# Two last iterations of a gated cross-attention block: Wo products in two parts, residual to quantised x by pairs of row tiles, moments of twelve score tiles on ScalarE

## The chip, the cores and the metric

The kernel runs on one core of one Trainium2 chip. The metric is the device time of one execution in microseconds; a row's times are counted from the start of the span of the profiled execution.

## The reference

Eight batches of x and of a context, 512 rows by 512 columns each, float32. Per batch: a layer norm of x, cross-attention with 16 heads of 32 to the context, an output projection, a gated residual, a second layer norm, and a feed-forward layer of 2048 hidden columns with quantised activations and ternary weights. Every head has a temperature of its own, which a small network makes from three features of its scores: mean, mean row maximum, and mean variance of the softmax rows.

```python
x = x + jnp.tanh(g_xattn[0]) * _L0_xattn_ref(_layernorm(x, axis=-1), ctx_1024, ctx_1024, ...)
x = x + jnp.tanh(g_ffn[0]) * _L0_ffn_ref(_layernorm(x, axis=-1), L0_ffn_w1, L0_ffn_w2)
# in _L0_xattn_ref
scores = qk / math.sqrt(dk)
probs = jax.nn.softmax(scores, axis=-1)
entropy_proxy = jnp.var(probs, axis=-1, ddof=1).mean(axis=-1)
...
attn_scores = qk / (2.0 * t)
attn = jax.nn.softmax(attn_scores, axis=-1)
return _linear(out, Wo, bo)
# in _L0_ffn_ref
scale = 127.0 / jnp.clip(jnp.max(jnp.abs(x), axis=-1, keepdims=True), EPS, None)
xq = jnp.clip(jnp.round(x * scale), -128.0, 127.0) / scale
h = jax.nn.gelu(_bitlinear(x, w1), approximate=False)
return _bitlinear(h, w2)
```

## The kernel before

The batches run through three stages that lie beside each other. Iteration i works on batch i + 1 (`has_p`: projections to q, k, v), on batch i (`has_a`: the scores once, for the features; 16 heads by 4 row tiles, 64 "score tiles" of 128 by 512) and on batch i - 1 (`has_b`: the scores again with the temperature, the values, Wo, residual, feed-forward). There are ten iterations, -1 to 8. Iteration 7 has no projections. Iteration 8 has only `has_b`, for the last batch.

Each engine has its own program, in the order in which `body` writes it; an instruction waits on semaphores for the others, and whatever is behind it on its engine waits too. Nothing but this written order decides what comes first.

A score tile is a TensorE product into one of four banks `a_ps` (`score_a`), a row maximum on VectorE (`row_max`, L925), an exponential on ScalarE into one of three slots of `etile` (`first_exp`, L738), and mean and variance of it on VectorE (`row_stat`, L930). The next product into a bank waits for the exponential of four tiles before. `A_PLAN_7` says how many of the 64 tiles of iteration 7 lie in its first part, among the attention of batch 6 ("sets", 48), and how many at each of 16 points behind it. `features` needs all moments.

Behind the sets comes, for batch i - 1:

- `normalise(i - 1, 3, ...)` on VectorE reads out the last chunk of outputs (`o_ps`, L947) and denominators (`z_ps`, L950) and turns the inverse (L957). `split_y` on GpSimd scales the chunk and splits it in two float16 halves, `yT`. There are four chunks, and chunks 0 to 2 were made during the sets.
- The Wo products: for each of four row tiles 12 matmuls (4 chunks, 3 pairs of halves, L1274) and one for the bias (L1277), into banks `b_ps`, `b_ps`, `o_ps`, `z_ps`. TensorE waits for all four chunks ahead of the first.
- `residual` (L1013), `residual_stat` (L986), aggregation (L1202), the reciprocal root on GpSimd (`inverse_deviation`, L621, L623), `norm_residual` (L993), `quantise_x` (L998 to L1004). From the aggregation on each step takes all four row tiles at once.
- Turning the quantised rows on TensorE (L1441), copying them out (row tiles 0 and 2 on VectorE, L1069, 1 and 3 on ScalarE, L839), and the up products of row tile 0 and 1 (`up`, L1450), four banks each of four matmuls, with a Gelu on ScalarE for each (L863). The first Gelu has a table load ahead of it.
- `scale_h` (L1079 and small ones) and `quantise_h` (L1093) on VectorE, turning, down products (L1485), `result` (L1108), and a store of each row tile.

## Time and profile before

| | |
|---|---|
| time, median of 3 runs | 1380.33 us (1379.63 to 1380.57) |
| the profiled execution's own time | 1382.32 us |
| its span | 1380.5 us |
| mean granted TensorE clock | 0.949 |
| busy: PE, DVE, ACT, POOL | 86%, 80%, 67%, 31% |
| chain that ended last | PE 50%, DVE 27%, issue 10%, ACT 8% |

The busy share is a mean over the whole span. A timeline row has the start, the length, the engine (PE is TensorE's matmul, DVE VectorE, ACT ScalarE, POOL GpSimd), the line, the operation with output and input, the count, and in brackets how long the engine was idle just before, and who ended it. Instructions overlap a little, so the distance of two starts is a better price than a length. `region` stands for several buffers.

### The profile page before, as it was taken

The numbers are of one execution on the slowest core, as the hardware profiler recorded it, in microseconds if no ns is written. First come the engines' busy times: TensorE is split into PE (matmuls) and PEld (weight loads), VectorE is DVE, ScalarE is ACT, GpSimd is POOL, SyncE is SP. The second block draws the span as 40 slices with busy tenths as digits, with TensorE's granted clock in tenths as the row PEclk, the third lists the DMA queues.
The fourth block names the chain that finished last, engine by engine and source line by source line (L and its number), as shares of the span: only waits on it lengthen the run. The fifth ranks groups of instructions, "written<-read, shape, count | busy, mean of one in ns | idle before, by whom it ended". The sixth has DMA issues, their size and how long they took to land.

```text
span 1380.5 us, 23490 instructions
## 1 busy us (share of the span) xinstructions
PE 1193.1 (86%) x6684; PEld 440.3 (32%) x6684; DVE 1103.3 (80%) x2054; ACT 922.7 (67%) x1527; POOL 421.9 (31%) x399
## 2 busy tenths in 40 slices
PE   5736669999989899999999999999999999869958
PEld 2202321344214431344224432344224431233224
DVE  6298779988798969897898969897898879983246
ACT  4463579756885769765985669664985679636713
POOL 4279474520253124510253124510353101100210
PEclk9857879999999999999999999999999999979979
DMA  8710221122112221012212221112112210001000
GB/s 295 227 51 11 62 68 38 36 46 62 61 48 47 47 71 54 22 28 62 62 47 47 47 79 47 28 32 58 55 47 46 55 54 1 1 1 62 1 0 31
DMA packets 35473, 73.70 MB, mean 53 GB/s; under 512 B 7952, under 2 KB 7952, under 8 KB 34832
## 3 DMA queue, kind: packets, MB, share of 16 engines
...
## 4 chain that ended last, share of the span: by engine, by line
PE 50%; DVE 27%; issue 10%; ACT 8%; POOL 1%; SPq 1%; DMA 1%; DVEq 1%; ACTq 0%; POOLq 0%
PE b_ps L1274 11%; DVE stat L930 7%; PE o_ps L1485 6%; DVE nmax L925 5%; PE o_ps L1274 5%; PE o_ps L1314 4%; PE z_ps L1274 4%; ACT region L755 4%; PE a_ps L1295 4%; PE b_ps L1301 4%; ACT etile L738 3%; DVE hmax L1079 2%; PE z_ps L1485 2%; PE b_ps L1450 2%; PE z_ps L1325 2%
## 5 line engine op out<-in xcount | busy, mean ns | idle before, releaser
L738 ACT ACTIVATE etile<-a_ps,nmax 128x512 f32<-128x512 f32 x512 | 368.2, 731 | 141.9 <-DVE nmax L925 141.6
L755 ACT ACTIVATE region<-b_ps,inv2t 128x512 f32<-128x512 f32 x512 | 353.3, 754 | 50.0 <-PE b_ps L1301 45.9
L925 DVE TENSOR_REDUCE nmax<-a_ps 128x1 f32<-128x512 f32 x512 | 345.7, 677 | 41.7 <-PE a_ps L1295 37.9
L930 DVE BATCH_NORM_STATS2 stat<-etile 128x6 f32<-128x512 f32 x512 | 347.8, 682 | 12.7 <-ACT etile L738 12.3
L1295 PE MATMUL a_ps<-kst,qst 96*128 96x512 f16 x512 | 202.8, 401 | 60.8 <-ACT etile L738 49.8
L1301 PE MATMUL b_ps<-qst,kst 97*128 97x512 f16 x512 | 192.6, 388 | 20.5 <-DVE region L1102 7.7
L1314 PE MATMUL o_ps<-region,vbuf 128*32 128x512 f32 x1024 | 137.9, 606 | 13.0 <-ACT region L755 7.0
L1325 PE MATMUL z_ps<-region,ones 128*32 128x512 f32 x1024 | 136.2, 604 | 8.4 <-DVE region L950 8.4
L1301 PEld LDWEIGHTS b_ps<-qst,kst 97*128 97x128 f16 x512 | 49.1, 96 | 290.2 <-ACT region L755 258.3
L655 POOL TENSOR_TENSOR region<-region 128x512 f16<-128x512 f32 x64 | 76.0, 1188 | 203.9 <-ACT region L788 203.7
L611 POOL TENSOR_TENSOR region<-region 128x512 f32<-128x512 f32 x32 | 40.8, 1276 | 292.0 <-DVE region L957 292.0
L1079 DVE TENSOR_REDUCE hmax<-region 128x1 f32<-128x512 f32 x128 | 82.2, 680 | 19.5 <-ACT region L863 18.2
L584 POOL CAST c_hi<-cin 128x512 f16<-128x512 f32 x28 | 17.1, 610 | 240.3 <-DMA cin<-in_ctxT_dram 239.5
L1295 PEld LDWEIGHTS a_ps<-kst,qst 96*128 96x128 f16 x512 | 50.7, 100 | 111.9 <-ACT etile L738 57.9
L1485 PE MATMUL o_ps<-f,region 128*128 128x512 fp8e4 x352 | 79.6, 379 | 0.0
L1450 PE MATMUL b_ps<-f,region 128*128 128x512 fp8e4 x256 | 65.3, 394 | 14.8 <-DVE region L1102 12.8
L863 ACT ACTIVATE region<-b_ps,xmax 128x512 f32<-128x512 f32 x64 | 43.4, 689 | 28.1 <-PE b_ps L1450 27.7
L632 POOL TENSOR_SCALAR cin<-cin,mv,rstd 128x512 f32<-128x512 f32 x28 | 57.9, 2077 | 2.8 <-POOL rstd L623 2.6
L873 ACT ACTIVATE region<-b_ps 128x1024 f16<-128x1024 f16 x31 | 31.7, 1023 | 32.0 <-PE b_ps L1461 31.2
L947 DVE TENSOR_SCALAR region<-o_ps 128x512 f32<-128x512 f32 x32 | 21.7, 680 | 36.9 <-PE o_ps L1314 36.9
L621 POOL TENSOR_SCALAR rstd<-mv 128x2 f32<-128x2 f32 (+1 forms) x23 | 5.3, 232 | 143.4 <-DVE mv L1202 87.4
L1274 PE MATMUL b_ps<-wo_hi,region 128*128 128x512 f16 x128 | 43.4, 399 | 5.7 <-POOL region L616 5.7
...
## 6 DMA issues: line engine op xcount, KB each, us to landing
kst<-region SPq DMA_DIRECT2D x96, 128.0 KB, 2.3
qst<-region SPq DMA_DIRECT2D x96, 128.0 KB, 2.3
...
```

The costliest lines, as they stand in the source:

```text
L738: nc.scalar.activation(etile[:, k % E_SLOTS, :], a_ps[k % A_BANKS][:, :], ACT.Exp, bias=nmax[:, slot_of(n), t:t + 1], scale=1.0).then_inc( ...
L755: nc.scalar.activation(probs[:, (s + 1) % 2, g, :], b_ps[g % 2][:, :], ACT.Exp, scale=inv2t[:, slot:slot + 1]).then_inc(b_exp, 1)
L925: vec.tensor_reduce(nmax[:, slot_of(k // T), k % T:k % T + 1], a_ps[k % A_BANKS][:, :], AX.X, ALU.max, negate=True).then_inc(a_max, 1)
L930: vec.bn_stats(stat[:, slot_of(k // T) * T + k % T, :], etile[:, k % E_SLOTS, :]).then_inc(a_stat, 1)
L1079: ins = vec.tensor_reduce(hmax[:, n:n + 1], hbuf[t % 2][:, n * S:(n + 1) * S], AX.X, ALU.max, apply_absolute_value=True)
L1274: ins = mat(mm_ps[bank_n][:, :], left[l](c), right[r](c), start=(c, l, r) == pairs[0], stop=bias is None and (c, l, r) == pairs[-1])
L1295: mat(a_ps[k % A_BANKS][:, :], qst[par][0:SHIFT, slot, t * P:(t + 1) * P], kst[par][0:SHIFT, slot, :], start=True, stop=True).then_inc(a_f ...
L1301: mat(b_ps[g % 2][:, :], kst[par][0:SHIFT + 1, slot, k * P:(k + 1) * P], qst[par][0:SHIFT + 1, slot, :], start=True, stop=True).then_inc(b ...
L1314: ins = mat(o_ps[g * DK:(g + 1) * DK, :], vbuf[par][:, k, n * DK:(n + 1) * DK], probs[:, (s + 1) % 2, g, :], start=k == 0, stop=k == T - 1)
L1325: ins = mat(z_ps[g * DK:(g + 1) * DK, :], ones32[:, 0:DK], probs[:, (s + 1) % 2, g, :], start=k == 0, stop=k == T - 1)
L1450: ins = mat(mm_ps[bank_n][:, :], xqT[:, c, t * P:(t + 1) * P], f1[:, c, n * S:(n + 1) * S], start=c == 0, stop=c == C - 1)
L1485: ins = mat(mm_ps[bank_n][:, :], hT[t % 2][:, k, :], f2[:, k, :], start=k == 0, stop=k == KC - 1)
```

## The change

It touches iterations 7 and 8 alone.

1. The Wo products of both iterations come in parts. `w_part(t, chunks)` makes chunks 0 to 2 of row tiles 0, 1 and 2 as soon as these chunks are there; then, when the last is, the rest of tiles 0 and 1, all of tile 3, and the rest of tile 2.
2. In iteration 7 the 16 tiles behind the sets move from points 0 to 7, two each, to the first six points, as 3, 3, 3, 3, 2, 2. The first nine of them now stand between the parts.
3. Residual to quantised x goes by pairs of row tiles (`stat_pair`, `quantise_pair`; the reciprocal root too). Turning pair 0 and its copies stand ahead of the up products of row tile 0, those of pair 1 ahead of the up products of row tile 1. ScalarE makes all four copies.
4. Moments of the last twelve tiles of batch 7 (`by_act`): ScalarE sums the exponentials as it makes them and squares them in place with a sum; three small VectorE instructions (`stats_by_act`) put mean and square sum where `features` reads them.
5. In iteration 8 a Gelu of a small, unused tile stands behind the last exponential.

```diff
@@ -50,16 +50,25 @@
-A_PLAN_7 = (48, (2, 2, 2, 2, 2, 2, 2, 2, 0, 0, 0, 0, 0, 0, 0, 0))
+A_PLAN_7 = (48, (3, 3, 3, 3, 2, 2, 0, 0, 0, 0, 0, 0, 0, 0, 0, 0))
...
+def by_act(i, k):
+    return isinstance(i, int) and (i == 7 and k >= H * T - 3 * T)
+BY_ACT = sum(by_act(7, k) for k in range(H * T))
...
+LINKS_END = 12
@@ -735,15 +753,33 @@
+                if k >= E_SLOTS and by_act(b, k - E_SLOTS):
+                    act_waits.wait_ge(squared, squares_by(b, k - E_SLOTS))
+                at = slot_of(n) * T + t
...
-                                     bias=nmax[:, slot_of(n), t:t + 1], scale=1.0).then_inc(a_exp, 1)
+                                     bias=nmax[:, slot_of(n), t:t + 1], scale=1.0,
+                                     accum_out=stat[:, at, 1:2] if by_act(b, k) else None).then_inc(a_exp, 1)
+            def squares_by(b, k):
+                return sum(by_act(b, n) for n in range(k + 1))
+            def square(b, k):
+                at = slot_of(k // T) * T + k % T
+                act_waits.wait_ge(a_exp, nth(b, H * T, k + 1))
+                nc.scalar.activation(etile[:, k % E_SLOTS, :], etile[:, k % E_SLOTS, :], ACT.Square,
+                                     accum_out=stat[:, at, 2:3]).then_inc(squared, 1)
             def late_exp(b, k):
...
+                if k > E_LATE and by_act(b, k - E_LATE - 1):
+                    square(b, k - E_LATE - 1)
...
+                    for late in range(H * T - E_LATE - 1, H * T):
+                        if by_act(b, late):
+                            square(b, late)
@@ -873,9 +912,14 @@
+                if has_b and not has_a:
+                    nc.scalar.activation(expt[:, :], expt[:, :], ACT.Gelu)
...
-                    gelus(0)
-                    gelus(1)
+                    for t in range(2):
+                        if not has_p:
+                            turned_xq(2 * t)
+                            turned_xq(2 * t + 1)
+                        gelus(t)
@@ -926,8 +970,25 @@
             def row_stat(b, k):
+                if by_act(b, k):
+                    return
+                covered = 1
+                while k + covered < H * T and by_act(b, k + covered):
+                    covered += 1
...
-                vec.bn_stats(stat[:, slot_of(k // T) * T + k % T, :], etile[:, k % E_SLOTS, :]).then_inc(a_stat, 1)
+                vec.bn_stats(stat[:, slot_of(k // T) * T + k % T, :], etile[:, k % E_SLOTS, :]).then_inc(a_stat, covered)
+            def stats_by_act(i):
+                by_tile = stat[:, :, :].rearrange("p (h t) f -> p h t f", t=T)
+                own = by_tile[:, 2 * C - 1::C, :, :]
+                mean, mean_too, rest = (own[:, :, :, f] for f in (1, 4, 5))
+                dve_waits.wait_ge(squared, BY_ACT)
+                vec.tensor_scalar(mean, mean, 1.0 / S, None, ALU.mult).then_inc(act_link, 1)
+                dve_waits.wait_ge(act_link, 1)
+                vec.tensor_copy(mean_too, mean)
+                vec.scalar_tensor_tensor(out=rest, in0=mean, scalar=-float(S), in1=mean,
+                                         op0=ALU.mult, op1=ALU.mult).then_inc(act_link, 1)
+                dve_waits.wait_ge(act_link, 2)
@@ -1005,6 +1066,31 @@
+            def stat_pair(i, pair, c):
+                for t in (2 * pair, 2 * pair + 1):
+                    ins = residual_stat(i, t)
+                c.link(ins)
+                for t in (2 * pair, 2 * pair + 1):
+                    ins = vec.bn_aggr(mv2[:, t, :], st6[:, t, :])
+                ins.then_inc(mv2_pair, 1)
+            def quantise_pair(i, pair, c):
+                cols = slice(2 * pair, 2 * pair + 2)
+                dve_waits.wait_ge(mv2_pair, nth(i - 8, 2, pair + 1))
+                dve_waits.wait_ge(rstd2_pair, nth(i - 8, 2, pair + 1))
+                for t in (2 * pair, 2 * pair + 1):
+                    ins = vec.tensor_scalar(xq[:, t, :], xres[:, t, :], mv2[:, t, 0:1], rstd2[:, t:t + 1],
+                                            ALU.subtract, ALU.mult)
+                c.link(ins)
+                c.link(vec.tensor_reduce(xmax[:, 0, cols], xq[:, cols, :], AX.X, ALU.max, apply_absolute_value=True))
+                c.link(vec.tensor_scalar(xmax[:, 0, cols], xmax[:, 0, cols], EPS, None, ALU.max))
+                vec.tensor_scalar(xmax[:, 3, cols], xmax[:, 0, cols], s1_127[:, 0:1], None, ALU.mult)
+                c.link(vec.reciprocal(xmax[:, 1, cols], xmax[:, 0, cols]))
+                c.link(vec.tensor_scalar(xmax[:, 2, cols], xmax[:, 1, cols], 127.0, None, ALU.mult))
+                for t in (2 * pair, 2 * pair + 1):
+                    vec.tensor_scalar(xq[:, t, :], xq[:, t, :], xmax[:, 2, t:t + 1], MAGIC,
+                                      ALU.mult, ALU.add).then_inc(xq_done, 1)
@@ -1089,6 +1175,9 @@
+                    dve_waits.wait_ge(mm_full[bank_n], before + 1)
+                elif not stages(i)[2]:
+                    bank_n, before = mm_use(i, "xq", T - 1)
@@ -1187,15 +1276,28 @@
-                if has_b:
+                if has_b and has_p:
...
-                for t in range(T):
+                elif has_b:
+                    c = Chain(dve_waits, end_link, LINKS_END, i - 8)
+                    residual(i, 0)
+                    residual(i, 1)
+                    stat_pair(i, 0, c)
+                    residual(i, 2)
+                    tiles_a(C)
+                    quantise_pair(i, 0, c)
+                    residual(i, 3)
+                    stat_pair(i, 1, c)
+                    tiles_a(C + 1)
+                    quantise_pair(i, 1, c)
+                    c.end()
+                for t in range(T) if has_p or not has_b else ():
...
-                if has_b:
+                if has_b and has_p:
@@ -1363,17 +1467,41 @@
-                    if has_b and n == 2:
+                    if has_b and has_p and n == 2:
...
-                    else:
+                    elif not has_b:
...
-                if has_b:
+                def w_part(t, chunks):
+                    bank_n = take(i, "W", t) if chunks[0] == 0 else mm_use(i, "W", t)[0]
+                    for c in chunks:
+                        for l, r in ((0, 0), (0, 1), (1, 0)):
+                            mat(mm_ps[bank_n][:, :], yT[:, l, c, t * P:(t + 1) * P], (w_hi, w_lo)[r]["o"][:, c, :],
+                                start=(c, l, r) == (0, 0, 0), stop=False)
+                    if chunks[-1] == C - 1:
+                        mat(mm_ps[bank_n][:, :], ones16[:, :], bias16[:, 1, :], start=False, stop=True) \
+                            .then_inc(mm_full[bank_n], 1)
+                if has_b and not has_p:
+                    pe_waits.wait_ge(y_done, nth(i - 1, C, C - 1))
+                    for t in range(T):
+                        if t == 2:
+                            pe_waits.wait_ge(o_out, nth(i - 1, C, C))
+                            pe_waits.wait_ge(z_out, nth(i - 1, C, C))
+                        if t == T - 1:
+                            pe_waits.wait_ge(y_done, nth(i - 1, C, C))
+                            w_part(0, (C - 1,))
+                            w_part(1, (C - 1,))
+                        w_part(t, range(C - 1) if t < T - 1 else range(C))
+                        alone(tiles_a(t))
+                    w_part(T - 2, (C - 1,))
+                    alone(tiles_a(C) + tiles_a(C + 1))
+                elif has_b:
...
-                for t in range(T):
+                for t in range(T) if has_p or not has_b else ():
@@ -1486,12 +1617,17 @@
-                    for t in range(T):
+                    for t in range(T) if has_p else ():
...
-                    up(0)
-                    up(1)
+                    for t in range(2):
+                        if not has_p:
+                            turned_xq(2 * t)
+                            turned_xq(2 * t + 1)
+                            drained(i, "xq", 2 * t)
+                            drained(i, "xq", 2 * t + 1)
+                        up(t)
```

TensorE's program in iteration 7, from the last denominators (`z_ps`) of the sets on; `a_ps` is a score tile, `b_ps0` with `wo` the Wo product of row tile 0. Before:

```order
L1325 MATMUL z_ps<-region1,ones32 32x512 x4
L1295 MATMUL a_ps0<-kst1,qst1 128x512
L1295 MATMUL a_ps1<-kst1,qst1 128x512
L1295 MATMUL a_ps2<-kst1,qst1 128x512
L1295 MATMUL a_ps3<-kst1,qst1 128x512
L1295 MATMUL a_ps0<-kst1,qst1 128x512
L1295 MATMUL a_ps1<-kst1,qst1 128x512
L1295 MATMUL a_ps2<-kst1,qst1 128x512
L1295 MATMUL a_ps3<-kst1,qst1 128x512
L1295 MATMUL a_ps0<-kst1,qst1 128x512
L1274 MATMUL b_ps0<-wo_hi,region4 128x512
L1274 MATMUL b_ps0<-wo_lo,region4 128x512
```
and now:

```order
L1429 MATMUL z_ps<-region1,ones32 32x512 x4
L1482 MATMUL b_ps0<-wo_hi,region4 128x512
L1482 MATMUL b_ps0<-wo_lo,region4 128x512
L1482 MATMUL b_ps0<-wo_hi,region4 128x512 x2
L1482 MATMUL b_ps0<-wo_lo,region4 128x512
L1482 MATMUL b_ps0<-wo_hi,region4 128x512 x2
L1482 MATMUL b_ps0<-wo_lo,region4 128x512
L1482 MATMUL b_ps0<-wo_hi,region4 128x512
L1399 MATMUL a_ps0<-kst1,qst1 128x512
L1399 MATMUL a_ps1<-kst1,qst1 128x512
L1399 MATMUL a_ps2<-kst1,qst1 128x512
L1482 MATMUL b_ps1<-wo_hi,region4 128x512
```
Nine matmuls of Wo have moved ahead of the first of these score tiles, and the tiles stand in threes between the parts.

ScalarE's program in iteration 7, its end of the score tiles up to the first Gelus; `etile` from `a_ps` is an exponential, `etile` from `etile` a square, `region3` a copy of turned x, `region4` a Gelu. Before:

```order
L738 ACTIVATE etile<-a_ps2,nmax 128x512
L738 ACTIVATE etile<-a_ps3,nmax 128x512
L839 ACTIVATE region3<-b_ps1 128x4x128
L839 ACTIVATE region3<-z_ps 128x4x128
L863 ACT_TABLE_LOAD
L863 ACTIVATE region4<-b_ps0,xmax 128x512
```
and now:

```order
L759 ACTIVATE etile,stat<-a_ps2,nmax 128x512
L769 ACTIVATE etile,stat<-etile 128x512
L759 ACTIVATE etile,stat<-a_ps3,nmax 128x512
L769 ACTIVATE etile,stat<-etile 128x512 x2
L856 ACTIVATE region3<-b_ps0 128x4x128
L856 ACTIVATE region3<-b_ps1 128x4x128
L902 ACT_TABLE_LOAD
L902 ACTIVATE region4<-o_ps,xmax 128x512
L902 ACTIVATE region4<-z_ps,xmax 128x512
L902 ACTIVATE region4<-b_ps0,xmax 128x512
L902 ACTIVATE region4<-b_ps1,xmax 128x512
```
Each tile has gained a square, behind the exponential of the next one, and all of these stand ahead of the copies. There is one table load, where it was.

VectorE's program in iteration 8, from the first residual on. Before:

```order
L1013 SCALAR_TENSOR_TENSOR xres<-b_ps0,tg_w,xres 128x512
L1013 SCALAR_TENSOR_TENSOR xres<-b_ps1,tg_w,xres 128x512
L986 BN_STATS st6<-xres 128x6
L1013 SCALAR_TENSOR_TENSOR xres<-o_ps,tg_w,xres 128x512
L986 BN_STATS st6<-xres 128x6
L1013 SCALAR_TENSOR_TENSOR xres<-z_ps,tg_w,xres 128x512
L986 BN_STATS st6<-xres 128x6 x2
L1202 BN_AGGR mv2<-st6 128x2 x4
L993 TENSOR_SCALAR region1<-xres,mv2,rstd2 128x512 x4
L998 TENSOR_REDUCE xmax<-region1 128x4
L999 TENSOR_SCALAR xmax<-xmax 128x4
L1000 TENSOR_SCALAR xmax<-xmax,s1_127 128x4
```
and now:

```order
L1099 SCALAR_TENSOR_TENSOR xres<-b_ps0,tg_w,xres 128x512
L1099 SCALAR_TENSOR_TENSOR xres<-b_ps1,tg_w,xres 128x512
L1047 BN_STATS st6<-xres 128x6 x2
L1074 BN_AGGR mv2<-st6 128x2 x2
L1099 SCALAR_TENSOR_TENSOR xres<-o_ps,tg_w,xres 128x512
L1082 TENSOR_SCALAR region1<-xres,mv2,rstd2 128x512 x2
L1085 TENSOR_REDUCE xmax<-region1 128x2
L1086 TENSOR_SCALAR xmax<-xmax 128x2
L1087 TENSOR_SCALAR xmax<-xmax,s1_127 128x2
L1088 RECIPROCAL xmax<-xmax 128x2
L1089 TENSOR_SCALAR xmax<-xmax 128x2
L1091 TENSOR_SCALAR region1<-region1,xmax 128x512 x2
```
The four residuals and four moments ahead of the aggregation have become two and two, the third residual stands between the first pair's aggregation and its normalising, and maximum and rounding take two row tiles.

## Rows read from the trace of the kernel before

**Rows 1.** Busy time in two stretches: length, PE, PEld, DVE, ACT, POOL, PEclk, DMA
```profile
1184.00:1212.00 28.00, 18.34 (x76) 6.90 (x68) 26.93 (x50) 10.99 (x16) 3.58 (x5) 0.84 0.00 1
1309.00:1342.00 33.00, 16.77 (x79) 7.47 (x72) 15.59 (x33) 2.48 (x3) 4.29 (x5) 0.76 0.00 0
```

**Rows 2.** Timeline of DVE, iteration 7: start, length, engine, line, operation, count, idle before
```profile
1186.11 0.69 DVE L925 TENSOR_REDUCE nmax<-a_ps 128x1 f32<-128x512 f32 x1
...
1188.51 0.69 DVE L957 STREAM_TRANSPOSE region<-zinv 128x512 f32<-128x512 f32 x1
...
1208.93 0.73 DVE L1013 SCALAR_TENSOR_TENSOR xres<-z_ps,tg_w,xres 128x512 f32<-128x512 f32 x1
1209.59 1.27 DVE L986 BATCH_NORM_STATS2 st<-xres 128x6 f32<-128x512 f32 x2
1210.89 0.38 DVE L1202 BATCH_NORM_AGGREGATE mv<-st 128x2 f32<-128x6 f32 x4
1212.83 1.91 DVE L993 TENSOR_SCALAR region<-xres,mv,rstd 128x512 f32<-128x512 f32 x4 [1.55 <-POOL rstd L623]
1214.78 2.29 DVE L998 TENSOR_REDUCE xmax<-region 128x4 f32<-128x2048 f32 x1
...
1217.85 1.67 DVE L1004 TENSOR_SCALAR region<-region,xmax 128x512 f32<-128x512 f32 x4
...
1234.70 1.29 DVE L1093 TENSOR_SCALAR region<-region,hsc 128x2048 f32<-128x2048 f32 x1
```

**Rows 3.** Timeline of PE, iteration 7
```profile
1184.52 1.04 PE L1295 MATMUL a_ps<-kst,qst 96*128 96x512 f16 x4
...
1221.23 3.57 PE L1450 MATMUL b_ps<-f,region 128*128 128x512 fp8e4 x8 [0.95 <-DVE region L1069]
```

**Rows 4.** Timeline of ACT, iteration 7
```profile
1220.32 0.60 ACT L839 ACTIVATE region<-z_ps 128x512 f16<-128x512 f16 x1 [0.26 <-PE z_ps L1441]
1220.93 1.28 ACT L863 ACT_TABLE_LOAD   x1
```

**Rows 5.** Timeline of ACT, iteration 6: an activation whose sum is read back
```profile
1031.74 0.69 ACT L784 ACTIVATE region<-b_ps,bqk 128x512 f32<-128x512 f32 x1
1032.32 0.19 ACT L784 ACTIVATION_READ_ACCUMULATOR region<-b_ps,bqk 128x1 f32 x1
1032.42 0.68 ACT L788 ACTIVATE region<-b_ps,bqk 128x512 f16<-128x512 f32 x1
```

**Rows 6.** Timeline of PE, iteration 8
```profile
1308.56 1.04 PE L1325 MATMUL z_ps<-region,ones 128*32 128x512 f32 x8
1315.34 0.58 PE L1274 MATMUL b_ps<-wo_hi,region 128*128 128x512 f16 x1 [5.74 <-POOL region L616]
...
1328.29 0.38 PE L1277 MATMUL z_ps<-bias,ones 128*128 128x512 f16 x1
...
1341.04 3.57 PE L1450 MATMUL b_ps<-f,region 128*128 128x512 fp8e4 x8 [0.98 <-DVE region L1069]
...
1373.65 3.62 PE L1485 MATMUL z_ps<-f,region 128*128 128x512 fp8e4 x16
```

**Rows 7.** Timeline of all engines, iteration 8
```profile
1311.13 0.71 DVE L957 STREAM_TRANSPOSE region<-zinv 128x512 f32<-128x512 f32 x1
...
1347.43 0.69 ACT L863 ACTIVATE region<-z_ps,xmax 128x512 f32<-128x512 f32 x1 [0.39 <-PE z_ps L1450]
...
1349.76 1.29 DVE L1093 TENSOR_SCALAR region<-region,hsc 128x2048 f32<-128x2048 f32 x1
...
1354.34 1.29 DVE L1093 TENSOR_SCALAR region<-region,hsc 128x2048 f32<-128x2048 f32 x1
```

**Rows 8.** TensorE's clock in stretches of 1 us (PEclk, third from the end)
```profile
1189.00:1190.00 1.00, 0.16 (x1) 0.00 (x0) 1.00 (x3) 0.18 (x1) 0.71 (x1) 0.80 0.00 0
...
1196.00:1197.00 1.00, 1.00 (x5) 0.44 (x4) 1.00 (x3) 0.50 (x2) 0.00 (x0) 0.79 0.00 0
1312.00:1313.00 1.00, 0.00 (x0) 0.00 (x0) 0.00 (x0) 0.00 (x0) 1.00 (x1) 0.74 0.00 0
```

53 lines of the change are left out of this document (34 added, 19 removed).

## The prediction

> **What bounds the kernel now.** I read the stages first, then each engine's timeline in them, and last the clock. Everything ahead of the last score tiles of iteration 7 keeps its instructions, so only two stretches matter.
>
> In iteration 7 the stretch from 1184 to 1212 is VectorE's: it is busy 26.93 of 28.00 us, ScalarE 10.99 [rows 1]. From 1186.11 it takes a maximum and a moment for each of 16 tiles, 0.60 us an instruction (four between 1186.11 and 1188.51), with the residual work between them. Then comes a chain with nothing beside it: aggregation at 1210.89, reciprocal root on GpSimd, normalising at 1212.83, maximum at 1214.78, rounding at 1217.85 [rows 2], turning, copying, and the first up product at 1221.23 [rows 3].
>
> In iteration 8 no engine is the bound from 1309 to 1342: TensorE 16.77, VectorE 15.59 of 33.00 us [rows 1]. It is one chain: denominators end about 1309.5, TensorE stands 5.74 us until GpSimd has split the last chunk of y, Wo runs 1315.34 to 1328.67, and the first up product starts at 1341.04 [rows 6]. The clock adds to it: it fell during 1312 to 1313 and Wo began at the lower level, 1.2 GHz, as did the up products (8 in 3.57 us against 16 in 3.62 us at the full 2.4 GHz) [rows 6, 8]. The chain from an up product to the rounding of h of tile 1 (1354.34) is the last place where the instructions differ in order; behind it TensorE runs nearly without gaps [rows 7].
>
> **The change in iteration 8**, on the clock of before. Three quarters of each of three Wo products, 27 matmuls at 0.216 us, 5.8 us, go into the gap from 1309.5: to 1315.3. TensorE has come straight from dense work, so I take the full clock. The last chunk is ready when it was, 4.21 us after the transposition at 1311.13, at 1315.34 [rows 6, 7]. Then 4, 4, 13 and 4 matmuls: tiles 0, 1, 3 and 2 are full at 1316.4, 1317.3, 1320.1 and 1320.9. The last was full at 1328.67: 7.8 us earlier.
>
> VectorE: residual of tiles 0 and 1 at 1316.5 and 1317.35 (0.66 each), moments 1.27 from 1318.0, two aggregations 0.2 to 1319.5. The root takes GpSimd and hand-overs 1.56 (1210.89 plus 0.38 to 1212.83) and is ready at 1321.05; residual 2 stands ahead in the order and waits for its bank until 1321.0, to 1321.65. Two normalisings 1.0, maximum of two tiles 1.2 (half of 2.29, a bound above is two row maxima of 0.69, 1.4), five small ones 0.8 (1214.78 plus 2.29 to 1217.85), rounding 0.5 and 0.9 [rows 2]: tile 1 is rounded at 1325.5. Turning takes 0.8 (rounded at 1219.52, the copy at 1220.32), ScalarE's copy 0.60, the hand-over 0.31 (1220.92 to 1221.23) [rows 2 to 4]: up product of tile 0 at 1327.2, against 1341.04: 13.8 earlier. TensorE was idle for over 4 us before, so I keep the half clock here.
>
> Now the price. Tile 1's up product waits for row tiles 2 and 3. They are rounded by 1333.0 (residual at 1325.4, then the same steps), hidden by the first up product; but their copies stand on ScalarE behind four Gelus. The fourth Gelu starts 6.39 us after the up product, as before (1341.04 to 1347.43), at 1333.6; two copies end at 1335.3; up product of tile 1 at 1335.6. Its 16 matmuls take 3.6, and from the start of the last Gelu to the rounding of h are 2.33 us (1347.43 to 1349.76) [rows 6, 7]: rounding of tile 1 at 1341.6 instead of 1354.34, **12.7 us** gained. Of 13.8 about 1.1 is given back. The dummy Gelu moves the 1.28 us table load behind the last exponential, where ScalarE waits some 15 us. I cost it at nothing and credit it with nothing: where it stood, the load ran beside the first up product, whose four matmuls take 1.9 us at the half clock [rows 4, 6]; at the full clock it would have been 0.3 late.
>
> **The change in iteration 7.** Nine Wo matmuls, 1.9 us, now stand ahead of tile 48, which started at 1184.52 [rows 3]; VectorE, free at 1186.11, gets it at 1186.9. That costs 0.8. Then six tiles with both instructions and two without moments until tile 56, at 1196.5; the transposition is at 1190.5, so the last y chunk is ready at 1194.7 (4.21 later). 21 matmuls, 4.5 us, stand before tile 57: VectorE gets it at 1199.55, having waited 3 us. Maxima 57 to 59, residuals 0 and 1, moments, aggregation, residual 2, maxima 60 and 61: 1206.1. Pair 0 is rounded at 1209.8, residual 3, moments and aggregation to 1211.9, and only then maximum 62, done at 1212.65, and 63.
>
> ScalarE's new work is twelve sums at exponentials and twelve squares. No square stands in the trace. An activation with its sum read back is followed by the next after 0.68 us (1031.74 to 1032.42) [rows 5]; the bounds are 0.60, the plain copy [rows 4], and 0.88, if 0.69 and 0.19 did not overlap. I take 0.68, the same shape. Twelve moments of 0.60 leave VectorE, 7.2 us; 16.3 us arrive on ScalarE, which had 17 idle. It is through tile 61's exponential by 1208 and waits for maximum 62 at any of these prices. Behind that are two exponentials and three squares, 3.4 us (3.1 to 4.4), to 1216.05, then two copies to 1217.15, and the up product at 1217.45: 3.8 earlier. As in iteration 8, copies 2 and 3 wait for four Gelus (1223.85), tile 1's up product starts at 1225.85, its rounding is at 1231.9 instead of 1234.70 [rows 2]: **2.8 us**. The three small VectorE instructions that finish ScalarE's moments, about 0.8, and the features end near 1221.7, before the Gelus need VectorE.
>
> Here the Trainium skill, in "ScalarE: Activation LUTs", What ACT_TABLE_LOAD costs, puts a switch at 2.66 us, a load of 1.28 and a drain of 1.38. The load agrees with the 1.28 of [rows 4]. By that figure, an estimate, the first Gelu of iteration 7 would start 0.45 us later, and the fourth, on which the sum rests, not at all.
>
> **Sum.** 12.7 and 2.8 are 15.5 us. The profiled execution took 1382.32 us (span 1380.5); 1366.8 then, and as the median of the runs was 2.0 lower, 1380.33, I predict **1364.8 us**.
>
> **Rivals.**
> - Both gains as above: 62%, 1362.8 to 1367.0, the width being the bounds of squares and maxima and a microsecond of where the clock rises.
> - The clock falls in iteration 7. Between 1191.7 and 1194.7 TensorE has only two score tiles, and with such sparse work it fell during 1189 to 1190, to rise during 1196 to 1197 after 3.4 us of dense work [rows 8]. 21 matmuls at half the clock for those 3.4 us cost 1.7 to 2.0 us, all ahead of tile 57 and so on the chain: 1366.8. For it: both falls came 3 to 4 us after dense work. Against: three bursts lie closer together now. 18%.
> - Iteration 7 gives nothing, because ScalarE's squares, its waits on itself and the late maximum 62 add up to 2.8 us more: 1367.6. 7%.
> - The clock is full at iteration 8's up product. The first Gelu then follows the copies, but rounding of tiles 2 and 3 (1333.0) holds the next: 1.0 more, 1363.8. 7%.
> - The Wo parts do not run ahead in iteration 8, held by a bank or by the fourth chunk: then only the pairs gain, 12.7 less 7.8: 1372.6. 3%. I see no such wait, the banks being read out by 1310.4.
> - Slower: the square needs another table than the exponential. From tile 53 on they alternate, 21 switches of 1.28 us are 27 us, less some 7 in which ScalarE waits: 20 onto the chain, 1385. From 18 switches on the kernel is slower. Against it: the instruction order has no load among them. 2%. By the 2.66 us a switch of the Trainium skill, "ScalarE: Activation LUTs", an estimate, it would be near 1414; the section Table sets: the hidden batching unit of the same page of the Trainium skill has the cheap functions in every set, and no run here shows a square yet.
> - The remaining 1% is no change.
>
> What a measurement of this kernel tells from none is 0.2%, 2.8 us: slower 2%, same 1%, faster 97%. 1361.5 to 1369.5 leaves out the last three cases and tails of the first.
>
> **What would show it.** Right: the first Wo matmul of iteration 8 directly behind the denominators, about 0.1 us instead of 5.74, and Wo at the full clock; last Wo product to first up product about 6.3 us instead of 12.4; in iteration 7 a ScalarE gap before the exponential of tile 62 and the up product 3.8 us earlier, but h of tile 1 only 2.8. Wrong: a square much over 0.7 us, table loads between L759 and L769, Wo matmuls 0.43 us apart in iteration 7, VectorE waiting over 4 us for tile 57, or a pair's chain longer than 4.0 us from normalising to the second rounding.

## The result, and the profile after

The changed kernel takes 1365.22 us (median of 4 runs, 1362.88 to 1366.75), the kernel before 1380.45 (4 runs beside it): ratio 0.9878, 95% interval 0.9862 to 0.9894. Of 1380.33 that is 16.8 us less (14.6 to 19.0); the medians differ by 15.2, which lies inside that. The prediction was 1364.8, range 1361.5 to 1369.5, a gain of 15.5. The profiled execution is the quickest of the four, 1362.88 us with a span of 1360.9, so its profile shows more gain than the median. One of the runs of parts_8 below, 1587.31 us at a granted clock of 0.745, is a slow one and is left out.

The same two stretches in the changed kernel; iteration 8's lies 6 us earlier. Columns as in [rows 1].

```profile
1184.00:1212.00 28.00, 16.43 (x73) 6.82 (x71) 23.80 (x49) 16.14 (x45) 4.91 (x7) 0.82 0.00 0
1303.00:1336.00 33.00, 26.11 (x136) 11.71 (x128) 24.57 (x57) 10.42 (x17) 4.92 (x7) 0.90 0.00 0
```

VectorE has 3.1 us less in the first stretch and ScalarE 5.2 more; in the second TensorE's busy share rose from half to four fifths, with the same length of window. Where the time went is seen in the timelines. First TensorE in iteration 8, the counterpart of [rows 6]:

```profile
1303.56 0.39 PE L1482 MATMUL b_ps<-wo_hi,region 128*128 128x512 f16 x1
...
1314.57 0.38 PE L1485 MATMUL o_ps<-bias,ones 128*128 128x512 f16 x1
1319.42 1.01 PE L1542 MATMUL b_ps<-ident,region 128*128 128x128 f16 x8 [4.47 <-DVE region L1091]
1321.23 1.86 PE L1581 MATMUL o_ps<-f,region 128*128 128x512 fp8e4 x4 [0.80 <-ACT region L856]
...
1328.47 1.89 PE L1581 MATMUL b_ps<-f,region 128*128 128x512 fp8e4 x8 [1.19 <-ACT region L856]
```

The 5.74 us of idle are gone: Wo follows the denominators directly (their last row starts at 1302.58 and Wo at 1303.56), 0.216 us a matmul throughout, and from its end (1314.95) to the first up product are 6.3 us. VectorE's timeline in the same place, the counterpart of [rows 7]:

```profile
1305.15 0.71 DVE L1018 STREAM_TRANSPOSE region<-zinv 128x512 f32<-128x512 f32 x1
...
1334.70 1.29 DVE L1182 TENSOR_SCALAR region<-region,hsc 128x2048 f32<-128x2048 f32 x1
```

ScalarE's timeline there:

```profile
1301.66 1.28 ACT L916 ACT_TABLE_LOAD   x1
...
1320.04 1.08 ACT L856 ACTIVATE region<-b_ps 128x512 f16<-128x512 f16 x2 [16.87 <-PE b_ps L1542]
...
1326.71 0.69 ACT L902 ACTIVATE region<-b_ps,xmax 128x512 f32<-128x512 f32 x1 [0.18 <-PE b_ps L1581]
```

The table load follows the last exponential; the unused Gelu comes behind it at 1302.96, and 16.87 us of waiting behind that. The copies of pair 1 stand behind the fourth Gelu, and TensorE waits 1.19 for them ahead of the up product of tile 1.

VectorE in iteration 7, against [rows 2]:

```profile
1182.44 0.69 DVE L1008 TENSOR_SCALAR region<-o_ps 128x512 f32<-128x512 f32 x1
...
1185.60 0.69 DVE L969 TENSOR_REDUCE nmax<-a_ps 128x1 f32<-128x512 f32 x1 [0.88 <-PE a_ps L1399]
...
1193.35 1.86 DVE L969 TENSOR_REDUCE nmax<-a_ps 128x1 f32<-128x512 f32 x3
1198.15 1.89 DVE L969 TENSOR_REDUCE nmax<-a_ps 128x1 f32<-128x512 f32 x3 [2.94 <-PE a_ps L1399]
...
1210.53 1.26 DVE L969 TENSOR_REDUCE nmax<-a_ps 128x1 f32<-128x512 f32 x2
...
1214.86 0.88 DVE L1091 TENSOR_SCALAR region<-region,xmax 128x512 f32<-128x512 f32 x2
1215.66 0.17 DVE L986 TENSOR_SCALAR stat<-stat 128x12 f32<-128x12 f32 x1
...
1228.72 1.29 DVE L1182 TENSOR_SCALAR region<-region,hsc 128x2048 f32<-128x2048 f32 x1
...
1235.27 0.68 DVE L1191 TENSOR_SCALAR region<-b_ps 128x1024 f16<-128x1024 f16 x1
```

It waits 2.94 us for tile 57 and makes the last two maxima at 1210.53. ScalarE there, against [rows 4, 5]: exponential with its sum, square with its sum, the late maximum, the copies and the table load.

```profile
1193.55 0.62 ACT L769 ACTIVATE etile<-etile 128x512 f32<-128x512 f32 x1
1194.07 0.19 ACT L769 ACTIVATION_READ_ACCUMULATOR etile<-etile 128x1 f32 x1
1194.16 0.68 ACT L759 ACTIVATE etile<-a_ps,nmax 128x512 f32<-128x512 f32 x1
...
1194.82 0.62 ACT L769 ACTIVATE etile<-etile 128x512 f32<-128x512 f32 x1
...
1211.22 0.69 ACT L759 ACTIVATE etile<-a_ps,nmax 128x512 f32<-128x512 f32 x1 [4.46 <-DVE nmax L969]
...
1214.40 1.07 ACT L856 ACTIVATE region<-b_ps 128x512 f16<-128x512 f16 x2
1215.49 1.28 ACT L902 ACT_TABLE_LOAD   x1
1217.48 0.69 ACT L902 ACTIVATE region<-o_ps,xmax 128x512 f32<-128x512 f32 x1 [0.70 <-PE o_ps L1581]
```

TensorE there, against [rows 3]:

```profile
1208.34 1.01 PE L1542 MATMUL b_ps<-ident,region 128*128 128x128 f16 x8 [5.46 <-DVE region L1091]
1215.57 1.86 PE L1581 MATMUL o_ps<-f,region 128*128 128x512 fp8e4 x4 [6.22 <-ACT region L856]
...
1222.74 1.89 PE L1581 MATMUL b_ps<-f,region 128*128 128x512 fp8e4 x8 [1.35 <-ACT region L856]
```

And the clock of the changed kernel, in stretches of 1 us (third figure from the end):

```profile
1196.00:1197.00 1.00, 1.00 (x6) 0.49 (x5) 0.00 (x0) 1.00 (x5) 0.00 (x0) 1.00 0.00 0
...
1202.00:1203.00 1.00, 0.61 (x1) 0.10 (x1) 0.96 (x4) 0.82 (x4) 0.07 (x1) 0.54 0.00 0
...
1219.00:1220.00 1.00, 1.00 (x6) 0.47 (x5) 0.93 (x4) 0.69 (x1) 0.00 (x0) 0.93 0.00 0
...
1324.00:1325.00 1.00, 1.00 (x4) 0.31 (x3) 1.00 (x1) 0.16 (x1) 0.00 (x0) 0.52 0.00 0
```

Two such stretches of the kernel before, where its clock rose:

```profile
1227.00:1228.00 1.00, 1.00 (x5) 0.39 (x4) 0.69 (x1) 0.44 (x2) 0.00 (x0) 0.93 0.00 0
...
1346.00:1347.00 1.00, 1.00 (x4) 0.39 (x3) 0.06 (x1) 0.64 (x1) 0.00 (x0) 0.69 0.00 0
```

It stayed at 2.4 GHz through iteration 7's Wo and fell to 1.2 at 1202.1, just ahead of the last score tile. The share of a stretch at the higher level gives the moment of a rise: 3.6 us (1219.1) and 3.7 us (1325.0) after the first up product began (1215.57, 1321.23); before, 5.9 and 5.6 (1227.1 and 1346.6 against 1221.23 and 1341.04). These differences do not belong to the change. In iteration 7 of only_8 and of parts_8, two kernels of the experiments that have the code of before there, the clock rose 5.5 us and 3.3 us after the up product (1222.26 and 1223.09). The stretch of parts_8:

```profile
1226.00:1227.00 1.00, 1.00 (x5) 0.44 (x4) 0.90 (x5) 0.37 (x1) 0.00 (x0) 0.81 0.00 0
```

**One measure for all runs.** The tail of iteration 7 begins at different times in runs of identical code ahead (1182.3 to 1187.4 in the fourteen profiles). So I count from VectorE's readout of the last chunk of y (the 1182.44 row; in iteration 8 the like one at 1302.83), in us: to the first up product, to the rounding of h of tile 1, and in iteration 7 to VectorE's copy of the second turned h (the 1235.27 row) and to TensorE's first scores for iteration 8. These are differences of starts in the timelines. "Rise" is how long after the first up product the clock rose to 2.4 GHz, from stretches of 0.1 us; "full" where it was there already. The kernels are those of the experiments.

| kernel | 7: up | rise | h of tile 1 | second copy | scores | 8: up | rise | h of tile 1 |
|---|---|---|---|---|---|---|---|---|
| before | 37.43 | 5.9 | 50.90 | 57.44 | 69.32 | 32.23 | 5.6 | 45.53 |
| changed | 33.13 | 3.6 | 46.28 | 52.83 | 64.70 | 18.40 | 3.7 | 31.87 |
| only_8 | 37.46 | 5.5 | 50.74 | 57.29 | 69.17 | 18.20 | 5.8 | 32.42 |
| only_7 | 33.13 | 4.0 | 46.49 | 53.04 | 64.92 | 33.01 | 3.0 | 45.04 |
| parts_8 | 37.69 | 3.3 | 49.86 | 56.41 | 68.45 | 25.72 | 3.8 | 38.13 |
| pairs_8 | 37.47 | 3.0 | 49.48 | 56.02 | 67.90 | 24.07 | full | 37.75 |
| dve_moments | 34.72 | 5.7 | 49.86 | 56.40 | 68.28 | 18.40 | 3.9 | 31.87 |
| four_early | 28.92 | 5.1 | 46.22 | 52.77 | 64.65 | 18.40 | 4.5 | 31.98 |
| busy_8 | 33.14 | 3.1 | 46.06 | 52.61 | 64.49 | 18.01 | full | 32.94 |
| best | 31.55 | full | 46.21 | 52.76 | 64.64 | 18.01 | full | 32.94 |
| late_3 | 28.90 | 4.5 | 46.22 | 54.16 | 67.28 | 18.39 | 4.6 | 32.06 |
| late_2 | 28.90 | 5.2 | 42.88 | 54.14 | 67.63 | 18.40 | 5.0 | 32.25 |
| late_1 | 33.14 | 3.6 | 46.27 | 57.53 | 70.64 | 18.40 | 4.6 | 32.06 |
| late_all | 28.91 | 5.2 | 42.87 | 52.58 | 65.61 | 18.40 | 3.6 | 31.88 |

So iteration 8 gained 13.66 us, iteration 7 4.62, and 1.36 of the spans' 19.6 is only that the tail began at 1182.44 and not 1183.80. Part of this is the clock's luck in this pair of profiles. Iteration 7's unchanged code gave 49.48 to 50.90 in four profiles, in the order of its rises (3.0, 3.3, 5.5, 5.9), and the changed code 46.06 to 46.49 in four (changed, only_7, busy_8, late_1), again in the order of the rises (3.1 to 4.0). The gain of iteration 7 is therefore 3.0 to 4.8, and 3.4 to 3.8 at like rises of 3.0 to 3.3; the changed order of iteration 7 was never seen with a late one. In iteration 8 the gain is 13.1 at late rises (before and only_8: 45.53 less 32.42) and 13.2 at early ones (only_7 and changed: 45.04 less 31.87). Together 16.5 to 17.0, which fits the 16.8 of the ratio.

### The profile page after: what moved, and what is told of

Read it like the earlier page. It is cut to its first block, busy times and chain, and to the rows that moved or that the text cites. A ratio compares the mean times of both kernels' runs of the same rounds, so it can differ in the third digit from the quotient of the medians.

```text
span 1360.9 us, 23535 instructions
## 1 busy us (share of the span) xinstructions
PE 1185.5 (87%) x6684; PEld 438.3 (32%) x6684; DVE 1097.6 (81%) x2051; ACT 932.9 (69%) x1568; POOL 424.0 (31%) x403
## 3 DMA queue, kind: packets, MB, share of 16 engines
q8 instruction: 62, 1.02, 0.3%
## 4 chain that ended last, share of the span: by engine, by line
PE 50%; DVE 27%; issue 10%; ACT 9%; POOL 1%; SPq 1%; DMA 1%; DVEq 1%; ACTq 0%; POOLq 0%
PE b_ps L1378 10%; DVE stat L979 7%; DVE nmax L969 6%; PE o_ps L1616 6%; PE o_ps L1378 5%; PE o_ps L1418 4%; ACT region L791 4%; PE b_ps L1405 4%; PE z_ps L1378 4%; PE a_ps L1399 4%; ACT etile L759 3%; DVE hmax L1165 2%; PE z_ps L1616 2%; PE z_ps L1429 2%; PE b_ps L1581 2%
## 5 line engine op out<-in xcount | busy, mean ns | idle before, releaser
L979 DVE BATCH_NORM_STATS2 stat<-etile 128x6 f32<-128x512 f32 x500 | 339.9, 683 | 12.5 <-ACT etile L759 12.1
L1165 DVE TENSOR_REDUCE hmax<-region 128x1 f32<-128x512 f32 x128 | 82.1, 680 | 12.7 <-ACT region L902 11.4
L1581 PE MATMUL b_ps<-f,region 128*128 128x512 fp8e4 x256 | 62.2, 380 | 14.3 <-DVE region L1191 11.7
L1616 PEld LDWEIGHTS o_ps<-f,region 128*128 128x128 f16 x352 | 33.8, 98 | 38.0 <-issue 1.1
```

The costliest lines, as they stand in the source:

```text
L979: vec.bn_stats(stat[:, slot_of(k // T) * T + k % T, :], etile[:, k % E_SLOTS, :]).then_inc(a_stat, covered)
L1165: ins = vec.tensor_reduce(hmax[:, n:n + 1], hbuf[t % 2][:, n * S:(n + 1) * S], AX.X, ALU.max, apply_absolute_value=True)
L1581: ins = mat(mm_ps[bank_n][:, :], xqT[:, c, t * P:(t + 1) * P], f1[:, c, n * S:(n + 1) * S], start=c == 0, stop=c == C - 1)
L1616: ins = mat(mm_ps[bank_n][:, :], hT[t % 2][:, k, :], f2[:, k, :], start=k == 0, stop=k == KC - 1)
```

## The experiments

Each is timed beside the kernel before, in four groups, each group on one chip: only_8, only_7, dve_moments and four_early; parts_8, pairs_8, busy_8 and best; late_3, late_2 and late_1; late_all. The ratio is to the kernel before of the same group, whose medians were 1382.41, 1382.01, 1382.53 and 1381.42 us. Gains in us are the ratio's of 1380.33. Each ratio has an interval of about 2 us either way, so differences between kernels of under 3 us rest on the table.

### Which iteration, which part

The edits are the changed kernel's parts behind switches: Wo in parts, pairs, point table, ScalarE's moments, the early Gelu.

```diff
-                if has_b and not has_p:
+                if parts(i):          # Wo in parts
...
-                if has_b and has_p:
+                if has_b and not pairs(i):   # whole residual, as before
...
-    return isinstance(i, int) and (i == 7 and k >= H * T - 3 * T)
+    return isinstance(i, int) and (i == 7 and k >= H * T - BY_ACT_HEADS * T)
# only_8:  table of before, IN_PARTS = (8,), IN_PAIRS = (8,), BY_ACT_HEADS = 0, early Gelu
# only_7:  new table, IN_PARTS = (7,), IN_PAIRS = (7,), BY_ACT_HEADS = 3, no early Gelu
# parts_8: table of before, IN_PARTS = (8,), IN_PAIRS = (), BY_ACT_HEADS = 0, no early Gelu
# pairs_8: table of before, IN_PARTS = (), IN_PAIRS = (8,), BY_ACT_HEADS = 0, no early Gelu
```

**only_8.** 

> Iteration 7 as before the change, iteration 8 as after it. By the prediction's sum iteration 8 holds 12.7 of the 15.5 us: 12.7 faster than before, 1367.7, or up to 1 us more where the clock rises early in the first up products, as it did in the profile of the changed kernel. Rival: iteration 7 holds more than its 2.8 us, as that profile's 4.6 between the two readouts suggests, and iteration 8 under 11.5 of the measured 15.2. It also shows whether the two gains add: this run and the one with iteration 7 alone should together be faster than before by 15 to 16 us.

Measured: 1369.73 us, ratio 0.9907 (0.9891 to 0.9922), 12.8 us; iteration 8 by the table 13.1. Here the clock rose late, as in the kernel before, which is the case that the prediction was worked out for: the up product came 14.0 earlier, the fourth Gelu 6.48 us behind it (1327.85 to 1334.33; forecast 6.39), and 0.9 was given back (forecast 1.1).

**only_7.** 

> Iteration 7 as after the change, iteration 8 as before it. Prediction's sum: 2.8 us faster than before, 1377.6; with the clock rising 1.7 us earlier in the up products, as in the profile of the changed kernel, 4.5 us, 1375.9. Rival: the squares on ScalarE and the late maximum of tile 62 eat it up, 0 to 1 us faster, 1380.

Measured: 1377.61 us, ratio 0.9968 (0.9954 to 0.9983), 4.4 us; by the table 4.4. The two add up: 17.2 of the change's 16.8.

**parts_8.** 

> The kernel before with one thing of the change: in iteration 8 the Wo products in parts. Neither pairs nor the early Gelu. The last product is full 7.8 us earlier by the prediction, but all four steps still wait for it, in the order 0, 1, 3, 2, so residual 2 and its moment come behind it: 7.8 to 8.0 us faster than before, 1372.5. Rival: the 27 matmuls that run ahead do not run at the full clock, 1.9 to 4 us less: about 1375.

Measured: 1374.19 us (five runs), ratio 0.994 (0.9926 to 0.9954), 8.3 us; by the table 7.4. The last Wo product is full 7.7 us earlier, but the first up product comes only 6.5 earlier: residual 2 now waits for that product, and it and its moment stand ahead of residual 3 and the aggregation, 1.26 us that the kernel before had hidden beside Wo (TensorE stands 10.76 us ahead of turning, before 9.50). That h of tile 1 still gains 7.4 is the early rise of the clock (3.8 against 5.6); against iteration 8 of only_7, with a rise at 3.0, it is 6.9.

**pairs_8.** 

> The kernel before with one thing of the change: in iteration 8 residual to quantised x by pairs, and all copies on ScalarE. Wo as before, so it is full at 1320.25, 1323.06, 1325.86, 1328.67. Pair 0 starts 5.6 us before the last product and is through before it; pair 1 starts where all four did, takes about 1.5 us less on VectorE, and its copies stand behind four Gelus. By adding: 12.7 less 7.8 is 4.9 us faster, 1375.5. If pairs in Wo's old, slower order let pair 0 run wholly beside Wo, the gain is larger, 6 to 7 us, and the parts and the pairs do not add. Rival: nothing, since the last copy, not the first, starts the feed-forward: 1379 to 1380.

Measured: 1374.19 us, ratio 0.9946 (0.9932 to 0.996), 7.5 us; by the table 7.8, where 4.9 was what my sum left for it. The parts alone and the pairs alone make 15.2, both together 13.7, or 14.2 and 13.2 against iteration 8 of only_7, where the clock rose early too. The timelines of TensorE show the difference. With parts alone, the first up product:

```profile
1332.42 1.03 PE L1567 MATMUL b_ps<-ident,region 128*128 128x128 f16 x8 [10.76 <-DVE region L1090]
...
1335.26 3.57 PE L1606 MATMUL b_ps<-f,region 128*128 128x512 fp8e4 x8 [0.95 <-DVE region L1180]
```

With pairs alone:

```profile
1330.86 0.61 PE L1567 MATMUL b_ps<-ident,region 128*128 128x128 f16 x8 [1.67 <-DVE region L1116]
...
1332.46 1.02 PE L1606 MATMUL o_ps<-f,region 128*128 128x512 fp8e4 x4 [1.00 <-ACT region L881]
```

With pairs alone the residual of pair 0 hides beside Wo's later tiles, TensorE stands only 1.67 us and the up product runs at the full clock (4 matmuls in 1.02 us); with the parts too, Wo is over sooner, TensorE stands 4.47 and the up product runs at half (1.86). Each part takes something that the other would also have given. The early Gelu has no run of its own, so that it gives nothing is argued and not shown.

### ScalarE's moments

```diff
-    return isinstance(i, int) and (i == 7 and k >= H * T - 3 * T)
+    return isinstance(i, int) and (i == 7 and k >= H * T - BY_ACT_HEADS * T)   # BY_ACT_HEADS = 0: no tile
```

**dve_moments.** 

> The changed kernel with all 64 moments of batch 7 on VectorE again: no sums at exponentials, no squares. Theory: VectorE gets 12 moments of 0.60 back; three hide in its wait for tile 57, nine do not, and those ahead of tile 62 delay the last exponentials, behind which the copies stand; five sums and squares fewer stand behind tile 62. Net 1.9 us slower than the changed kernel, 1367.1. Rival: the squares stand on the chain themselves (three of 0.62 behind tile 62's maximum) and moving moments gained nothing: 0 to 1 us faster than the changed kernel.

Measured: 1368.73 us, ratio 0.9898 (0.9884 to 0.9913), against 0.9878 of the change: 2.8 us slower, and 3.6 in iteration 7 by the table. The 2.8 alone would not be clear of noise; beside four_early, timed on the same chip, its five runs (1366.84 to 1371.90) all lie above those four (1362.98 to 1366.25). With its moments on VectorE iteration 7 has 49.86, inside the 49.48 to 50.90 of the unchanged one: parts and pairs alone give it 0 to 1 us, though the up product comes 2.7 earlier. Its gain is the work that left VectorE. It is less than the 7.2 us of the twelve moments, since part of them hides in VectorE's waits: that for tile 57 is 1.15 us here against 2.94, those for Gelus are gone, and the small three are not needed.

### The late maximum and the clock

```diff
-A_PLAN_7 = (48, (3, 3, 3, 3, 2, 2, 0, 0, 0, 0, 0, 0, 0, 0, 0, 0))
+A_PLAN_7 = (48, (3, 3, 3, 3, 4, 0, 0, 0, 0, 0, 0, 0, 0, 0, 0, 0))
```

**four_early.** 

> The changed kernel with the last four score tiles of batch 7 together, all ahead of the rounding of pair 0, instead of two there and two behind the aggregation of pair 1. Theory: what holds the first up product of iteration 7 is the maximum of tile 62 (ScalarE idle 4.46 us in the profile, then two exponentials and three squares, then the copies). The pair 0 chain gets 1.2 us longer, ScalarE is through before it, the first up product starts about 3.5 us earlier and that of tile 1 about 2.8: 1362.4. Rival: VectorE's own chain is the bound, 1.2 us slower than the changed kernel, 1366.4.

Measured: 1365.0 us, ratio 0.9877 (0.9861 to 0.9893): as the change. The first up product came 4.2 us earlier, and h of tile 1 was rounded at 46.22 against 46.28. My reason, the late maximum as the bound, fell. VectorE shows what held it: behind the rounding of pair 1 come features and both tiles' maxima of h with no idle time, and TensorE waits for it. VectorE's timeline in four_early:

```profile
1224.10 1.29 DVE L1207 TENSOR_SCALAR region<-region,hsc 128x2048 f32<-128x2048 f32 x1
1225.30 2.46 DVE L1190 TENSOR_REDUCE hmax<-region 128x1 f32<-128x512 f32 x4
...
1228.68 1.29 DVE L1207 TENSOR_SCALAR region<-region,hsc 128x2048 f32<-128x2048 f32 x1
```

TensorE's timeline there, behind the up product of tile 1:

```profile
1225.44 1.07 PE L1617 MATMUL b_ps<-ident,region 128*128 128x128 f16 x16 [2.56 <-DVE region L1207]
```

In the changed kernel two chains end almost together here: this one and ScalarE's Gelus behind the late copies, for which VectorE waits four times by 0.18 us. And four_early opens a wait of its own: the last two maxima no longer stand between the aggregation of pair 1 and its normalising, and VectorE waits 1.21 us there for GpSimd's root.

```profile
1213.06 1.00 DVE L1107 TENSOR_SCALAR region<-xres,mv,rstd 128x512 f32<-128x512 f32 x2 [1.21 <-POOL rstd L662]
```

```diff
...
+                            for n in range(WARM[i]):       # WARM = {8: 20}
+                                mat(a_ps[0][:, :], ident16[:, :], w_hi["o"][:, 0, :], start=True, stop=True)
...
                             turned_xq(2 * t)
```

**busy_8** adds these matmuls, whose results nobody reads, ahead of the first transposes of iteration 8. 

> The changed kernel, and in iteration 8 twenty more matmuls of 128 by 512 into an unused bank, between the last Wo product and the first turning, whose results nobody reads: 4.3 us at 2.4 GHz in a gap of 4.6. Theory: they keep the clock up, the first up products of iteration 8 run at 0.22 instead of 0.43 us a matmul, but the rounding of pair 1 then holds the up product of tile 1: 1.0 us faster, 1364.2, with less spread between runs. Rival: the clock at the first up products costs nothing that shows, or the added matmuls delay the turning: same to 1 us slower.

Measured: 1368.15 us, ratio 0.9891 (0.9875 to 0.9907), no gain (its five runs go from 1364.31 to 1368.68). TensorE:

```profile
1325.05 1.02 PE L1606 MATMUL o_ps<-f,region 128*128 128x512 fp8e4 x4 [0.82 <-ACT region L881]
...
1330.70 0.40 PE L1567 MATMUL o_ps<-ident,region 128*128 128x128 f16 x4 [2.04 <-DVE region L1116]
...
1332.32 3.57 PE L1606 MATMUL b_ps<-f,region 128*128 128x512 fp8e4 x8 [0.82 <-ACT region L881]
```

Tile 0's up product ran at the full clock, then TensorE stood 2.04 us for pair 1's rounding and 0.82 for a copy, the clock fell at 1332.3, and tile 1's up product ran at half: h of tile 1 at 32.94, 1.07 later than in the change. The half clock had been moved by one product. In pairs_8 the same two waits were 1.85 and 0.83 and the clock stayed up; what decides between them is open.

**best** joins four_early, busy_8 and 24 such matmuls in iteration 7. 

> The changed kernel with the last four score tiles together ahead of pair 0's rounding, and added matmuls ahead of the first turning in both iterations (24 in iteration 7, 20 in iteration 8). Theory: 2.8 us for the tiles, 1.0 for the clock in iteration 8 and up to 2.5 for it in iteration 7, where the first up products then run at the full clock and pair 1 becomes the bound: 1359 to 1361. Rival: the added matmuls collide with turning in iteration 7, where the gap depends on ScalarE: not better than the tiles alone.

Measured: 1365.19 us, ratio 0.9878 (0.9864 to 0.9892): as the change. In iteration 7 the rival was seen: the 24 matmuls took 7.52 us, and the first up product came 2.6 us later than in four_early, though at the full clock. Yet h of tile 1 was rounded at 46.21, as in four_early and the change. Over these three the up product lies anywhere from 28.92 to 33.13 and that rounding does not move: VectorE sets it.

### VectorE's order in iteration 7

If VectorE's order holds the tail, the 3.2 us of features, which only a small product needs, should be worth moving.

```diff
-                if has_a:
+                if has_a and not put_off:      # put_off: iteration 7
                     features(i, par)
                 if has_b:
                     scale_h(i, 0)
                     quantise_h(i, 0)
+                    if put_off:
+                        features(i, par)       # late_3; late_2 and late_1: behind quantise_h(i, 1)
```

**late_3.** 

> As four_early (the Gelus of iteration 7 start 4.2 us earlier than in the changed kernel), and VectorE makes the last squares' three small operations, the features and their reductions of iteration 7 (4.0 us, 1216.9 to 1220.7 in four_early) behind the rounding of h's first row tile in place of ahead of it. Theory: in four_early VectorE's order was the bound. Then the first row tile of h is rounded 4.0 us earlier, TensorE's 2.56 us of idle ahead of its transposes is gone, and the kernel takes 2 to 2.7 us less than four_early: about 1362.6 where the changed kernel takes 1365.2. Rival: something else ended late (the up products, or the later row tiles of h): no gain, 1365. Second rival: the features are late for their own product, which then costs as much as was won: 1365 to 1366, with an idle time of TensorE ahead of the product with w1r.

Measured: 1368.57 us, ratio 0.9904 (0.9889 to 0.9919): the scores of iteration 8 come 2.6 us later than in four_early.

**late_2.** 

> As late_3, but features and small operations stand behind the rounding of h's second row tile. Theory (VectorE's order): both roundings are 4 us earlier than in four_early, the features come about 1.4 us late for their product, and 1.0 to 1.5 us of late_3's 2 to 2.7 us are left: 1363.9. Rival: as four_early, 1365.

Measured: 1369.92 us, ratio 0.9905 (0.989 to 0.992).

**late_1.** 

> The changed kernel (its own tile order in iteration 7, Gelus not earlier), with the features behind the rounding of h's second row tile. There VectorE waits for the Gelus of the second row tile three times by 0.18 us and TensorE stands at its transposes without idle: two chains end together. Theory: to shorten one alone gives nothing, within 0.7 us of the changed kernel. Rival: VectorE's order was the only bound of iteration 7 there too: 2 us or more faster, 1363.

Measured: 1371.63 us, ratio 0.9922 (0.9908 to 0.9936), 6 us slower than the change. All three lost in one place, here late_3:

```profile
1230.43 1.89 PE L1609 MATMUL b_ps<-f,region 128*128 128x512 fp8e4 x4 [4.57 <-DVE region L1216]
...
1233.22 1.89 PE L1620 MATMUL b_ps<-ident,region 128*128 128x128 f16 x16
```

The fourth chunk of the third up product needs a bank that VectorE's copy of the first turned h frees. TensorE's idle 2.56 us became 4.57 us ahead of that chunk, and the 16 transposes behind took 1.89 us against 1.07: the clock had fallen. I had not counted that wait. In all three, as in the kernels that they start from, the features stand ahead of that copy. So in late_3 and late_2 the copy starts where it did in four_early (47.42, 47.41 and 47.42 us after the readout), and what was won ahead of it only lengthens TensorE's wait. In late_1 the copy comes 3.3 us later than in the change (50.81 against 47.48): there the features had lain in a time in which VectorE waits for the first Gelus anyway. Now VectorE stands idle for them (2.15, 0.94 and 0.24 us), and the features come on top.

```diff
                         turned_h(i, t, has_p)
+                        if put_off and t == 0:
+                            features(i, par)
...
+                        if put_off and t == 1:    # TensorE: behind down(0), ahead of up(3)
+                            first_products()
```

**late_all.** 

> As four_early, with VectorE's features of iteration 7 (3.2 us) behind its copy of the turned h of the first row tile, TensorE's two products that need them behind the first down product, and ScalarE's two operations on them behind its copy of the second turned tile. In late_3 TensorE's idle time only moved, by 3.8 us, to the fourth chunk of the third up product, whose bank that copy frees, and the clock fell there. Theory (VectorE's order up to that copy is the bound): the copy now comes 3.2 us earlier, the transposes of h's second row tile start some 3.9 us earlier than four_early's, those of the third some 3 to 3.7, and the kernel takes 2 to 3.7 us less than four_early and the changed kernel: 1361.5 to 1363.2 where the changed kernel takes 1365.2. Rival: the order costs nothing because another engine (ScalarE's Gelus, TensorE's products at a fallen clock) fills the tail: under 1 us. Second rival: the clock falls in a new idle time and takes 2 us or more back: 1365 to 1368.

Measured: 1364.41 us, ratio 0.9871 (0.9855 to 0.9887): not to be told from the change or from four_early. The roundings came 3.4 us earlier (42.87), as VectorE's order said, and again nothing reached the end. TensorE:

```profile
1229.13 1.04 PE L1621 MATMUL b_ps<-f,region 128*128 128x512 fp8e4 x4 [0.85 <-DVE region L1228]
...
1237.64 1.04 PE L1621 MATMUL z_ps<-f,region 128*128 128x512 fp8e4 x4 [2.56 <-DVE region L1228]
1238.52 3.24 PE L1621 MATMUL b_ps<-f,region 128*128 128x512 fp8e4 x8
```

It waits for VectorE's copy of the second turned h, and the clock falls behind that. The column "second copy" has the answer: 52.83 in the change, 52.77 in four_early, 52.58 here. In four_early and here VectorE works without idle time from pair 1's normalising to that copy (in four_early from 1213.06 to 1235.91), and the sum is the same: the 3.2 us of features only changed places, and with them went the 3.4. The second rival, a new idle time with a fallen clock, was seen behind that copy, and by the scores it cost 1.0 us more (65.61 against 64.65), which the times do not show.

## Why the prediction was right, step by step

- **Time.** 1364.8 against 1365.22; faster was forecast at 97%. The likeliest case held, with both gains somewhat too small: 12.7 and 2.8 against 13.1 to 13.7 and 3.0 to 4.8 in the profiles, 12.8 and 4.4 by the ratios of the two halves. That the median came within 0.4 us is closer than the working deserves, since the ratio puts the gain at 14.6 to 19.0.
- **Iteration 8, up product.** 13.8 us earlier forecast, 13.83 measured (14.0 in only_8); the last Wo product full 7.8 earlier, measured 7.7; last Wo product to up product 6.3 and 6.3.
- **Iteration 8, what is given back.** 1.1 forecast, 0.2 in the profile of the change and 0.9 in only_8. The term that differs is the fourth Gelu, 6.39 us after the up product: it came after 5.48 (1321.23 to 1326.71) where the clock rose after 3.7 us, and after 6.48 in only_8, where it rose after 5.8, as before (5.6). On the clock that it assumed the forecast was right to 0.4 us; which clock a run gets is luck.
- **The clock full at iteration 8's up product** (the 7% rival, 1.0 us more gained) did not come by itself, and where busy_8 forced it, h of tile 1 came 1.07 later: the rival had left out that the clock would fall again at tile 1's product.
- **"12.7 less 7.8" for the pairs alone** was a wrong split: 7.8 measured (7.3 against only_7). The gains overlap: with Wo's old length pair 0 hides beside it, and the up product finds the full clock.
- **Iteration 7, waits.** VectorE late for tile 57 by 3 us, measured 2.94; maximum 62 done at 1212.65, measured 1211.2 on a tail that began 1.36 earlier; a square at 0.68, measured 0.61 from start to the next start, a summed exponential 0.66; the small three 0.8, measured 0.5. The tile-48 delay was 0.8, measured 0.85 (its start after the readout 3.16, before 2.31).
- **Iteration 7, up product.** 3.8 earlier, measured 4.3.
- **Iteration 7, h of tile 1.** 2.8, measured 3.0 to 4.8. The mis-sized term is again the stretch from up product to h: 14.45 us forecast (1217.45 to 1231.9), 13.15 measured, and of these 1.3 us the fourth Gelu has 1.0 (5.40 after the up product, 1215.57 to 1220.97, where 6.39 was taken). More than the size was off: I gave the late maximum as what bounds it, and four_early, best and late_all showed VectorE's sum of work to bound it as closely. An up product 2.7 us earlier alone gave 0 to 1 us (dve_moments). The 7.2 us that left VectorE, which I had used only to place the maxima, are the source of the gain; that the sum through the up product came near it is in part luck.
- **Clock in iteration 7's Wo** (the 18% rival): no fall; the matmuls stand 0.216 us apart.
- **Table loads.** None between exponentials and squares, so the slower rival did not come. For the switch I weighed the 2.66 us of the Trainium skill, "ScalarE: Activation LUTs", What ACT_TABLE_LOAD costs: the trace doesn't agree in this place. The load took 1.28 from 1215.49 to 1216.77 and the Gelu began at 1217.48, 0.71 later and not 1.38, when its operand from TensorE was there; the unused Gelu at 1302.96 began 0.02 us after its load.
